# Implied waits left out on TensorE, two pieces of work exchanged, and a loop of four slots, in the second layer of an audio tower

## The chip, the cores and the metric

One Trainium2 chip, one core. The metric is the device time of one execution, in microseconds (us). The program is written in Bass: each engine (PE, the TensorE; DVE, the VectorE; ACT, the ScalarE; POOL, the GpSimd; SP, which issues the DMAs) has its own instruction stream, and the streams meet only at semaphores.

## The reference

The input is 64 sequences of 375 rows of 256 numbers. A first stage makes 188 tokens of each (a convolution of stride 2 and a layer norm), and a first layer adds attention and a quantised feed-forward part. The change touches only the second layer:

```python
q, k, v = heads(x @ wq.T), heads(x @ wk.T), heads(x @ wv.T)      # x is the layer-normed h; 16 heads of 64
phi = lambda t: exp(t @ omega.T - 0.5 * sum(t * t)) / sqrt(64)
out[n] = sum over m <= n of (phi(q)[n] . phi(k)[m]) v[m] / (sum over m <= n of phi(q)[n] . phi(k)[m] + 1e-6)
h = h + out @ wo.T + bo
y = silu(layernorm(layernorm(h)) @ w1 + b1)                     # 1024 columns, w1 and w2 dequantised
h = h + layernorm(h) + 0.5 * (y @ w2 + b2)
```

(The last two lines are in short: the feed-forward part takes the layer-normed h as its input and as its residual.)

## The kernel before

**Slots and chunks.** Layer 2 works on slots of two sequences (32 slots, `SLOTS`), 384 rows each. A slot has eight chunks (`CH`), a chunk being two heads. Chunks are numbered through, g = 8 s + c. Every engine runs the same skeleton, `slots(eng, step)` at L1106: slots -1 to 2 are written out, slots 3 to 28 run in a hardware loop of two slots an iteration (`nc.Fori`, L1116), and slots 29 to 34 are written out again (the last ones only finish work of earlier slots). In the loop the slot number is a register, so a semaphore count that depends on it is worked out by the engine's sequencer; in the written-out slots it is a constant.

**Software pipeline.** In the step of chunk g PE does, in this order (L1332): the omega product of g-1 (`c2_proj`, bank pair B), the q and k products of g (`c1_qk`, bank pair A), the scores of g-2 (`c3_scores`), a piece of "place" 0, the transposes of g-4 (`c5_transpose`), a piece of place 1, the product with V of g-3 (`c4_av`), and a piece of place 2. The pieces are the work that is not done chunk by chunk, and `places` (L1122) writes out by hand which stands where: v in place 0 of the even chunks, wo in place 0 of the odd ones, the eight fc1 pieces of slot s-2, the four fc2 pairs, and the two transposes h5 and xn. All pieces use the two halves of A, as the q and k products do.

**What a piece needs.** Before PE writes a half of A it waits in `bank_free` (L1177) for the last readers, which `read[i]` lists. An fc1 piece f fills both halves with two matmuls each (L1303, L1304). ACT turns half 0 into `pre` (L1405), DVE adds half 1 to it (L1515). One place later ACT takes the tanh (L1413) and DVE multiplies (the gelu-like product, L1522); two places later ACT rounds the result to yT_hi (the copy helper, L1356) and POOL subtracts to get yT_lo (L1594). An fc2 pair j needs both parts of pieces 2j and 2j+1, and DVE adds its result to the rows (L1500). The wait for a pair stands in `fc2_pair` (L1320).

**Precision.** A product of split operands is three matmuls (`product3`, L928, so its lines are L930 to L932): high by low, low by high, high by high. For each chunk ACT copies q and k (qk_hi, twice), DVE subtracts (qk_lo, L1447), ACT squares both (L1365, which counts on qk_hi too), copies the squares (sqs_hi), and POOL subtracts (sqs_lo, L1636, 128x768). The squares are ACT's last reading of A, and they wait for qk_lo.

**Loops of the first layer.** They have the same form (L394), with two tiles an iteration.

Of the kernel before, what the change touches and what calls it, by code (L numbers as in the profile page):

```python
# [16 lines left out]
KC = DM // 128  # L17
# [22 lines left out]
FC = F1 // 128  # L40
# [12 lines left out]
PAIR = 2 * 128  # L53
RING = 4


# [878 lines left out]
def layer1(nc, omega, bo, ln_g, ln_b, fc1_q, fc1_s, fc1_b, fc2_q, fc2_s, fc2_b, h2_dram, out, ident, eps, exponent,  # L935
           w1, w1_memory, w1_loaded):
    GCH = SLOTS * CH
    with ExitStack() as ctx:
# [167 lines left out]
        def slots(eng, step):  # L1106

            last = 3 + (SLOTS - 5) // 2 * 2

            def slot(s, par):  # L1110
                for c in range(CH):
                    step(s, c, par)

            for s in range(-1, 3):
                slot(s, s % 2)
            with nc.Fori(3, last, 2, engines=(eng.engine,), hint_back_edge=True) as s:  # L1116
                slot(s, 1)
                slot(s + 1, 0)
            for s in range(last, SLOTS + 3):
                slot(s, s % 2)  # L1120

        def places(s, par):  # L1122

            p = [[None] * 3 for _ in range(CH)]
            for j in range(4):
                p[2 * j][0] = ("v", s, j)
                p[(2 * j + 7) % CH][0] = ("wo", s if j == 0 else s - 1, j, par if j == 0 else 1 - par)
            for f, (c, n) in enumerate(((2, 1), (2, 2), (3, 1), (4, 1), (4, 2), (5, 2), (6, 1), (7, 2))):
                p[c][n] = ("fc1", s - 2, f)
            p[3][2], p[5][1] = ("fc2", s - 2, 0, par), ("fc2", s - 2, 1, par)  # L1130
            p[0][1], p[1][2] = ("fc2", s - 3, 2, 1 - par), ("fc2", s - 3, 3, 1 - par)
            p[1][1], p[7][1] = ("h5", s - 2), ("xn", s + 1)
            return p
# [13 lines left out]
        with nc.Block() as block:  # L1147
# [26 lines left out]
            def _(pe):  # L1174
# [7 lines left out]
                def c1_qk(s, c, g):  # L1182
                    if c == 0:
                        wait(pe, "xT_hi", s + 1, KC)
                        wait(pe, "xT_lo", s + 1, KC)
                    for i, w in enumerate((wq, wk)):
# [4 lines left out]
                        last.then_inc(S["qk_done"], 1)  # L1191
                        read[i].extend((("qk_hi", 4 * g + (3 + i)), ("qk_lo", 2 * g + (1 + i))))

                def c2_proj(g):

                    wait_g(pe, "qk_lo", g + 1, 2)
                    wait_g(pe, "sq_lo", g + 1)
# [8 lines left out]
                def c3_scores(g, b):  # L1206
                    wait_g(pe, "phi_ready", g + 1)
                    wait_g(pe, "aT_ready", g)
# [16 lines left out]
                def c4_av(g, b, sg, c):  # L1225
                    wait_g(pe, "aT_ready", g + 1)
                    wait_g(pe, "att1_step", g, 3)
                    if c % 2 == 0:
# [22 lines left out]
                def c5_transpose(g):  # L1251
                    wait_g(pe, "att1_step", g + 1, 3)
                    wait_g(pe, "attT_hi", g)
                    wait_g(pe, "attT_lo", g)
# [24 lines left out]
                def xn_transpose(s):  # L1279
# [6 lines left out]
                    for k in range(KC):  # L1286
                        read[k].extend((("xT_hi", s * 2 + (k + 1)), ("xT_lo", s * 2 + (k + 1))))

                def h5_transpose(s):
                    wait(pe, "h5_gb", s + 1, 2)  # L1290
                    transpose_rows(x4, "hT_transposed")
                    for k in range(KC):
                        read[k].extend((("hT_hi", s * 2 + (k + 1)), ("hT_lo", s * 2 + (k + 1))))

                def fc1(s, f):

                    if f == 0:
                        wait(pe, "hT_hi", s + 1, KC)
                        wait(pe, "hT_lo", s + 1, KC)
# [20 lines left out]
                def fc2_pair(s, j, par):  # L1320
                    pe.wait_ge(S["y_hi"], s * FC + (2 * j + 2))
                    pe.wait_ge(S["y_lo"], s * FC + (2 * j + 2))
                    rows_product(s, yT, fc2, j, "fc2_done", "out_ready")

                def wo_pair(s, j, par):
                    pe.wait_ge(S["attT_hi"], s * CH + (2 * j + 2))
                    pe.wait_ge(S["attT_lo"], s * CH + (2 * j + 2))
# [362 lines left out]
```

## Time and profile before

| | |
|---|---|
| time of the runs | 4787.19, 4795.0, 4800.82 us (median 4795.0) |
| the profiled execution | 4793.58 us by its own time, span 4791.8 us, mean granted clock 0.98 |
| PE busy | 93% of the span |
| PE weight loads | 83% |
| DVE, ACT, POOL busy | 71%, 52%, 39% |
| chain that ended last | PE 45%, issue 9%, POOL 5%, DVE 2%, ACT 1% |

The profile is that of one execution. PE is the engine of the matmuls; PEld is its weight loads, which run beside the matmuls before them. Matmuls are pipelined, so a matmul's duration is longer than the distance from its start to the next one's: 0.28 us and 0.12 us for the common 256-column matmul. "issue" as a releaser means that the engine waited for nothing that the profile shows, its sequencer apart. An entry with a q behind the engine's name belongs to its sequencer: branches, register work, waits. An idle time in square brackets is the time that the engine stood still before that row, with what ended it. A cause named for a wait on several semaphores is the one that came last by the profile. The granted clock is a share of 2.4 GHz; the lower level is 1.2 GHz.

### The profile page before, as it was taken

Reading aid. Unit: us, or ns where it says so; the run is one execution under the profiler, and the core shown is the slowest. Engines: PE = TensorE matmul, PEld = TensorE weight load, DVE = VectorE, ACT = ScalarE, POOL = GpSimd, SP = SyncE. Lnnn points to the kernel's source line nnn. Section 1 sums busy time; section 2 is a strip of 40 time slices with the busy share of each in tenths; the row PEclk is TensorE's granted clock in tenths of the full one; section 3 lists DMA queues with packets and bytes.
Section 4 is the critical chain, followed back from the end, with each engine's and each line's share of the span. In section 5 each row is a group of like instructions: output and inputs, shape, how many; then the busy total and the mean of one; then the engine's idle time right before and its main releaser. Section 6 shows DMA issues by size and latency. Waiting matters only on the chain.

```text
span 4791.8 us, 120275 instructions
## 1 busy us (share of the span) xinstructions
PE 4454.1 (93%) x43016; PEld 3973.3 (83%) x43016; DVE 3397.0 (71%) x7197; ACT 2495.3 (52%) x5314; POOL 1855.2 (39%) x2018
## 2 busy tenths in 40 slices
PE   3999999999999948999999999999999999999997
PEld 2888888888888847888888888888888888888886
DVE  5899999999999853666666666665666666666665
ACT  2555555555555524555554554554555555555553
POOL 1444444444444422343343343333334333334333
PEclk9999999999999979999999999999999999999998
DMA  2000000000000010000000000000000000000000
GB/s 82 19 23 23 23 23 23 23 23 23 23 23 23 22 41 8 5 15 8 8 11 11 8 8 15 8 8 15 8 8 11 11 8 8 14 8 8 15 5 11
DMA packets 64881, 78.93 MB, mean 16 GB/s; under 512 B 8759, under 2 KB 51127, under 8 KB 64439
## 3 DMA queue, kind: packets, MB, share of 16 engines
q1 hardware_dynamic: 64566, 74.07, 5.4%
q8 instruction: 279, 4.57, 0.4%
q14 instruction: 36, 0.29, 0.0%
HBM read 49.40 MB, written 24.64 MB: 15 GB/s over the span
## 4 chain that ended last, share of the span: by engine, by line
PE 45%; issue 9%; POOL 5%; DVE 2%; ACT 1%; POOLq 0%; DMA 0%; DVEq 0%; ACTq 0%; SPq 0%
PE bA L930 9%; PE bA L931 8%; PE bA L932 8%; PE bS L1216 3%; PE bO L1239 2%; PE bA L1303 2%; PE bB L930 2%; POOL sqs_lo L1636 2%; PE bB L1202 2%; PE bB L932 2%; PE bB L931 2%; PE bB L1203 2%; PE bA L1304 1%; PE bT L1256 1%; POOL yT_lo L1594 1%
## 5 line engine op out<-in xcount | busy, mean ns | idle before, releaser
L1636 POOL TENSOR_TENSOR sqs_lo<-sq,sqs_hi 128x768 fp32r<-128x768 f32 x256 | 471.4, 1842 | 811.7 <-ACT sqs_hi L1356 803.9
L1447 DVE TENSOR_TENSOR qk_lo<-bA,qk_hi 128x384 fp32r<-128x384 f32 x512 | 283.4, 553 | 626.4 <-ACT qk_hi L1356 626.2
L1375 ACT ACTIVATE phi<-bB 128x768 f32<-128x768 f32 x256 | 207.9, 812 | 681.2 <-PE bB L1203 681.2
L1594 POOL TENSOR_TENSOR yT_lo<-tanh_y,yT_hi 128x384 fp32r<-128x384 f32 x256 | 258.2, 1009 | 631.2 <-ACT yT_hi L1356 631.2
L1356 ACT ACTIVATE qk_hi<-bA 128x384 fp32r<-128x384 f32 x512 | 251.2, 491 | 229.6 <-PE bA L932 229.6
L1457 DVE TENSOR_TENSOR aT<-bS,mask 128x1024 f32<-128x1024 f32 x256 | 310.9, 1215 | 1.8 <-PE bS L1221 1.6
L930 PE MATMUL bA<-fc_lo,yT_hi 128*128 128x256 f32 x768 | 231.5, 301 | 60.9 <-POOL yT_lo L1594 34.2
L1365 ACT ACTIVATE sq<-bA 128x384 f32<-128x384 f32 x512 | 250.2, 489 | 61.7 <-DVE qk_lo L1447 61.6
L516 PE MATMUL bank<-down_sb,hqT 128*128 128x256 f32 x1128 | 278.5, 389 | 1.0 <-ACT hqT L598 1.0
L614 ACT ACTIVATE kblk<-gu,kb_masked,rowmask 128x128 f32<-128x128 f32 x752 | 270.7, 462 | 6.3 <-PE gu L540 6.3
L516 PEld LDWEIGHTS bank<-down_sb,hqT 128*128 128x128 f32 x1128 | 204.4, 190 | 52.6 <-issue 32.6
L930 PE MATMUL bB<-qk_lo,omega_hi 128*128 128x384 f32 x512 | 184.2, 360 | 67.5 <-issue 64.9
L930 PE MATMUL bA<-wo_lo,attT_hi 128*128 128x256 f32 x768 | 226.8, 295 | 18.1 <-DVE qk_lo L1447 5.3
L930 PE MATMUL bA<-wv_lo,xT_hi 128*128 128x256 f32 x768 | 228.4, 297 | 13.2 <-ACT sq L1365 1.0
L1216 PE MATMUL bS<-phi 64*64 64x192 f32 x4096 | 226.5, 337 | 0.0
L1239 PE MATMUL bO<-V,aT 128*64 128x65 f32 x4096 | 219.4, 228 | 0.0
L931 PE MATMUL bA<-fc_hi,yT_lo 128*128 128x256 f32 x768 | 219.3, 286 | 0.0
L932 PE MATMUL bA<-fc_hi,yT_hi 128*128 128x256 f32 x768 | 219.3, 286 | 0.0
L1522 DVE SCALAR_TENSOR_TENSOR tanh_y<-tanh_y,pre 128x384 f32<-128x384 f32 x256 | 214.1, 836 | 6.5 <-ACT tanh_y L1413 6.5
L1303 PE MATMUL bA<-hT_lo,fc_w 128*128 128x384 f32 x512 | 211.7, 414 | 6.6 <-ACT pre L1405 5.4
L1405 ACT ACTIVATE pre<-bA,fc1b,fc1s 128x384 f32<-128x384 f32 x256 | 170.9, 668 | 89.7 <-PE bA L1304 89.6
L931 PE MATMUL bA<-wv_hi,xT_lo 128*128 128x256 f32 x768 | 215.5, 281 | 0.0
(243 smaller groups left out, 15025.4 us busy)
## 6 DMA issues: line engine op xcount, KB each, us to landing
xT<-in_x SPq DMA_DIRECT2D x94, 256.0 KB, 2.7
h_scratch<-h SPq DMA_DIRECT2D x188, 64.0 KB, 1.9
hx<-h_scratch SPq DMA_DIRECT2D x32, 256.0 KB, 2.7
out<-res SPq DMA_DIRECT2D x32, 256.0 KB, 2.1
hx<-h_scratch SPq DMA_DIRECT2D x64, 64.0 KB, 2.4
out<-res SPq DMA_DIRECT2D x64, 60.0 KB, 1.8
q<-in_fc_q SPq DMA_DIRECT2D x2, 1024.0 KB, 6.2
wq_sb<-in_wq SPq DMA_DIRECT2D x1, 1024.0 KB, 5.0
```

Source lines behind the costliest of these rows:

```text
L516: last = pe.matmul(cv[:, 0:DM], hqT[0:w, f, :], down_sb[0:w, f, :], start=f == 0, stop=f == len(F0C) - 1)
L614: act.activation(kblk[:, c, :, j, :], src, ACT.Identity, bias=kb_masked[:, c, j:j + 1], scale=rowmask[:, j:j + 1]).then_inc(S["qk_copied"], 1)
L930: pe.matmul(out, lhs[0], rhs[1], start=start, stop=False)
L931: pe.matmul(out, lhs[1], rhs[0], start=False, stop=False)
L932: return pe.matmul(out, lhs[0], rhs[0], start=False, stop=stop)
L1216: pe.matmul(SC[o:o + 64, h, q], phi[b][p, 1, k], phi[b][p, 0, q], start=True, stop=True)
L1239: pe.matmul(O[o:o + 64, dst(i)], aT[b][:, h, HEADS[i] + o:HEADS[i] + o + 64], V[:, i, v], start=True, stop=True)
L1303: pe.matmul(A[:, k, 0:NT], w, hT[1][:, k, :], start=True, stop=False)
L1447: dve.tensor_tensor(dst, src, hi.bitcast(fp32), ALU.subtract).then_inc(S[done], 1)
L1457: dve.tensor_tensor(aT[b][:], SC[:, :, 0:ST], mask[:].unsqueeze(1).broadcast_to([128, 2, ST]), ALU.mult)\
L1594: pool.tensor_tensor(yT[1][:, f % RING, :], tanh_y[f % 2][:], yT[0][:, f % RING, :].bitcast(fp32), ALU.subtract).then_inc(S["y_lo"], 1)
L1636: pool.tensor_tensor(sqs[1][:], sq[:], sqs[0][:].bitcast(fp32), ALU.subtract).then_inc(S["sq_lo"], 1)
```

## The change

Three things are done in the second layer.

1. The loop takes four slots an iteration. `last` becomes 27, so there are 6 iterations, and slots 27 and 28 are written out.
2. In `places` the fourth fc1 piece (f = 3) moves from chunk 4, place 1 to chunk 3, place 2, and the first fc2 pair moves the other way. The engines all read this table, so ACT, DVE and POOL move their share with it.
3. On PE, waits are left out where another wait of PE's, earlier or at the same place, cannot end before them: those for xT_hi, hT_hi, attT_hi and y_hi beside those for the low part, which is computed from the high one; qk_lo beside the later counts of qk_hi and sq_lo; phi_ready in the scores; and att1_step in the product with V.

```diff
+UNROLL = 4
...
-            last = 3 + (SLOTS - 5) // 2 * 2
+            last = 3 + (SLOTS - 5) // UNROLL * UNROLL
...
-            with nc.Fori(3, last, 2, engines=(eng.engine,), hint_back_edge=True) as s:
-                slot(s, 1)
-                slot(s + 1, 0)
+            with nc.Fori(3, last, UNROLL, engines=(eng.engine,), hint_back_edge=True) as s:
+                for u in range(UNROLL):
+                    slot(s + u, (1 + u) % 2)
...
-            for f, (c, n) in enumerate(((2, 1), (2, 2), (3, 1), (4, 1), (4, 2), (5, 2), (6, 1), (7, 2))):
+            for f, (c, n) in enumerate(((2, 1), (2, 2), (3, 1), (3, 2), (4, 2), (5, 2), (6, 1), (7, 2))):
                 p[c][n] = ("fc1", s - 2, f)
-            p[3][2], p[5][1] = ("fc2", s - 2, 0, par), ("fc2", s - 2, 1, par)
+            p[4][1], p[5][1] = ("fc2", s - 2, 0, par), ("fc2", s - 2, 1, par)
...
                 def c1_qk(s, c, g):
                     if c == 0:
-                        wait(pe, "xT_hi", s + 1, KC)
                         wait(pe, "xT_lo", s + 1, KC)
...
-                        read[i].extend((("qk_hi", 4 * g + (3 + i)), ("qk_lo", 2 * g + (1 + i))))
+                        read[i].append(("qk_hi", 4 * g + (3 + i)))
...
                 def c2_proj(g):
-                    wait_g(pe, "qk_lo", g + 1, 2)
                     wait_g(pe, "sq_lo", g + 1)
...
                 def c3_scores(g, b):
-                    wait_g(pe, "phi_ready", g + 1)
+                    if not has_chunk(g + 1):
+                        wait_g(pe, "phi_ready", g + 1)
                     wait_g(pe, "aT_ready", g)
...
                 def c4_av(g, b, sg, c):
                     wait_g(pe, "aT_ready", g + 1)
-                    wait_g(pe, "att1_step", g, 3)
...
                 def c5_transpose(g):
                     wait_g(pe, "att1_step", g + 1, 3)
-                    wait_g(pe, "attT_hi", g)
...
-                        read[k].extend((("xT_hi", s * 2 + (k + 1)), ("xT_lo", s * 2 + (k + 1))))
+                        read[k].append(("xT_lo", s * 2 + (k + 1)))
...
-                        read[k].extend((("hT_hi", s * 2 + (k + 1)), ("hT_lo", s * 2 + (k + 1))))
+                        read[k].append(("hT_lo", s * 2 + (k + 1)))
...
                     if f == 0:
-                        wait(pe, "hT_hi", s + 1, KC)
                         wait(pe, "hT_lo", s + 1, KC)
...
-                    pe.wait_ge(S["y_hi"], s * FC + (2 * j + 2))
                     pe.wait_ge(S["y_lo"], s * FC + (2 * j + 2))
...
-                    pe.wait_ge(S["attT_hi"], s * CH + (2 * j + 2))
                     pe.wait_ge(S["attT_lo"], s * CH + (2 * j + 2))
```

## Rows read from the trace of the kernel before

**Rows 1.** The page, its first part: busy time and instructions of each engine.

```profile
PE 4454.1 (93%) x43016; PEld 3973.3 (83%) x43016; DVE 3397.0 (71%) x7197; ACT 2495.3 (52%) x5314; POOL 1855.2 (39%) x2018
```

**Rows 2.** What PE waited for in the second layer: us in total, times, longest us.

```profile
PE bB L930 <- issue: 52.0, 48, 3.7
PE bA L930 <- POOL yT_lo L1594: 28.1, 17, 2.2
PE bA L930 <- DVE pre L1515: 22.9, 13, 1.8
```

**Rows 3.** L1116's branch: count, ns min/median/max, first and last start in us.

```profile
L1116 PEldq COMPARE_BRANCH  x13: 88/2137/3497, 2218.3 to 4428.0; - x13
...
L1116 DVEq COMPARE_BRANCH  x13: 55/61/68, 2219.5 to 4429.0; - x13
```

**Rows 4.** The first layer's loop branch, L394, on PE's queue.

```profile
L394 PEldq COMPARE_BRANCH  x42: 80/216/260, 210.7 to 1619.3; - x42
```

**Rows 5.** One loop iteration, second layer then first: busy (x instructions) PE, PEld, DVE, ACT, POOL.

```profile
2405.00:2587.30 182.30, 174.44 (x1816) 160.82 (x1816) 115.59 (x243) 93.30 (x176) 69.75 (x54) 0.99 0.04 10
...
245.50:279.30 33.80, 33.64 (x284) 28.57 (x282) 30.46 (x68) 19.98 (x52) 15.54 (x24) 1.00 0.09 23
```

**Rows 6.** PE in time (start us, us): first product of chunks 7 and 2, three crossings.

```profile
2208.15 0.41 PE L930 MATMUL bB<-qk_lo,omega_hi 128*128 128x384 f32 x1 [0.49 <-issue]
...
2245.43 0.34 PE L930 MATMUL bB<-qk_lo,omega_hi 128*128 128x384 f32 x1
...
2303.28 0.41 PE L930 MATMUL bB<-qk_lo,omega_hi 128*128 128x384 f32 x1 [0.51 <-issue]
...
2336.45 0.34 PE L930 MATMUL bB<-qk_lo,omega_hi 128*128 128x384 f32 x1
...
4233.35 0.41 PE L930 MATMUL bB<-qk_lo,omega_hi 128*128 128x384 f32 x1 [0.49 <-issue]
...
4272.03 0.34 PE L930 MATMUL bB<-qk_lo,omega_hi 128*128 128x384 f32 x1
```

**Rows 7.** The stretch at one edge; granted clock third from last.

```profile
2587.30:2598.00 10.70, 7.03 (x48) 5.83 (x46) 2.92 (x7) 2.79 (x5) 3.63 (x2) 0.84 0.02 5
```

**Rows 8.** PE in time, chunks 3 to 5 of one slot.

```profile
2535.87 0.29 PE L1221 MATMUL bS<-phi 64*64 64x64 f32 x8
2536.27 0.38 PE L930 MATMUL bA<-wo_lo,attT_hi 128*128 128x256 f32 x1
...
2540.59 0.29 PE L1248 MATMUL bO<-V,aT 128*64 128x65 f32 x4
2542.49 0.36 PE L930 MATMUL bA<-fc_lo,yT_hi 128*128 128x256 f32 x1 [1.61 <-POOL yT_lo L1594]
...
2544.62 0.34 PE L930 MATMUL bB<-qk_lo,omega_hi 128*128 128x384 f32 x1
...
2552.18 0.42 PE L1303 MATMUL bA<-hT_lo,fc_w 128*128 128x384 f32 x1
...
2553.16 0.45 PE L1239 MATMUL bO<-V,aT 128*64 128x65 f32 x8
...
2562.70 0.36 PE L930 MATMUL bA<-fc_lo,yT_hi 128*128 128x256 f32 x1
...
2564.99 0.45 PE L1239 MATMUL bO<-V,aT 128*64 128x65 f32 x8
```

**Rows 9.** PE in time, an unrolled slot: end of chunk 0's scores, start of its v.

```profile
4432.98 0.29 PE L1221 MATMUL bS<-phi 64*64 64x64 f32 x8
4433.31 0.39 PE L930 MATMUL bA<-wv_lo,xT_hi 128*128 128x256 f32 x1
```

**Rows 10.** DVE and ACT in time beside that chunk 3.

```profile
2539.04 1.72 DVE L1522 SCALAR_TENSOR_TENSOR tanh_y<-tanh_y,pre 128x384 f32<-128x384 f32 x1
...
2541.98 0.62 DVE L1515 SCALAR_TENSOR_TENSOR pre<-bA,fc1s,pre 128x384 f32<-128x384 f32 x1 [0.75 <-ACT pre L1405]
...
2541.22 0.65 ACT L1405 ACTIVATE pre<-bA,fc1b,fc1s 128x384 f32<-128x384 f32 x1
```

## The prediction

> **What bounds the kernel now.** I began with the page's busy times [rows 1]: PE is busy 4454.1 us of the span of 4791.8, no other engine over 71%. PE sets the end, and the gain must come from its idle time, its slow stretches and its order of work. The change touches only the second layer, from about 1860 us on. Next I read what PE waited for there [rows 2]. Two things stand out: 51.0 us (28.1 + 22.9, 30 times) ahead of an fc2 product, put down to POOL's yT_lo and to DVE's pre, and 52.0 us ahead of the omega product at a chunk's start, put down to "issue", which means that PE's own sequencer was late. The longest of these is 3.7 us. Third I read the loop's own instructions [rows 3]. PE's COMPARE_BRANCH takes 2137 ns in the median and up to 3497; the single short one, 88 ns, belongs to leaving the loop. On DVE it takes 61 ns. Last I went through single slots in order of time [rows 6, 8], as everything there repeats from slot to slot within a few hundredths of a us.
>
> **Part 1, four slots in an iteration.** There are 32 slots; the loop runs from slot 3 to 29 in 13 iterations, so PE jumps back 12 times. After the change it runs from 3 to 27 in 6 iterations and jumps back 5 times: 7 jumps fewer. To price a jump I measured from the first product of chunk 7 to that of chunk 2 in the next slot. Without a jump this takes 2336.45 - 2303.28 = 33.17 us. With one it takes 37.28 at the first jump and 38.68 at the last, so 4.1 and 5.5 us more [rows 6]. Over the 12 jumps the extra is 3.6 to 6.2, mean 4.9. That is more than the branch alone: the register work after it, a second short bubble in the chunk that follows, and at 8 of the 12 jumps a stretch at the lower clock (granted clock 0.84 over the 10.7 us that begin at one jump; of the two levels 1.2 and 2.4 GHz that is a mixture), while PE stood still for up to 3.7 us just before [rows 2, 7]. 7 x 4.9 = **34 us less**; ends 7 x 3.6 = 25 and 7 x 6.2 = 43. Slots 27 and 28 become unrolled code, which costs nothing: unrolled slots take as long as loop slots without a jump.
>
> A longer body could have a price of its own. One iteration holds 1816 matmuls and 1816 weight loads on PE, against 284 and 282 in the first layer's [rows 5], whose jump takes 216 ns [rows 4]. A small body jumps cheaply, a large one doesn't, and nothing in the rows says that it gets dearer once it is large. I take the five that stay at their present price.
>
> The Trainium skill has a rule that speaks against this part (Runtime: NRT & Kernel Launch, "Instruction fetch mechanics"): an engine holds 512 instructions, PE 2048, and a taken branch whose target is no longer held has to fetch it before the engine goes on. Both PE rows agree with it. By it the jumps of DVE and ACT, whose bodies double, would begin to stall as PE's do; that is the second rival below.
>
> **Part 2, waits left out.** Each wait that goes is implied by one that stays, so no order changes; what is saved is sequencer work, and only where PE stands still for it. That is one place in each chunk: the v or wo product after the scores, which needs bank A and so ACT's last read of it. There PE waits for qk_hi first and for qk_lo after it. In the loop 0.40 us lie between the last group of score matmuls and the wo product (2535.87 to 2536.27) [rows 8]. In an unrolled slot, where no count is worked out in a register, it is 0.33 us (4432.98 to 4433.31) [rows 9]. I take 0.07 us for a chunk in the loop, since with one wait left the count can be worked out before it is due. In chunks 3 and 6 the gain is lost again, as PE waits there for DVE or POOL anyway. So 6 chunks x 0.07 x 24 loop slots = 10 us, and about 5 us for the wo products of the 8 unrolled slots, which drop two waits: **15 us less**. Ends: nothing at all, if the instruction that works out the count still stands ahead of the weight load, and 25 us, if waits ahead of fc1 and the omega product were also costing a little.
>
> The waits ahead of the scores, the av product and the transposes are passed while the matmuls before them still run, at no time of PE's. Left out they give nothing; had they hidden work, nothing would be late, since the engine queue is full.
>
> **Part 3, fc2's first pair and fc1's fourth piece change places.** In chunk 3 the fc2 pair follows the av product with 1.61 us of idle [rows 8]. It needs yT_lo of piece 1, which comes by a chain: DVE's gelu product on tanh_y ends at 2540.76 (2539.04 + 1.72) [rows 10], then ACT rounds it, and then POOL subtracts. After the change fc1's piece 3 stands there. It needs no yT, but it needs bank A, which fc1's piece 2 has just filled: half 0 is free when ACT's pre ends, 2541.22 + 0.65 = 2541.87, half 1 when DVE's pre ends, 2541.98 + 0.62 = 2542.60 [rows 10]. ACT's pre stands behind the rounding of the same piece 1, so the chain only loses its last link. The first matmul comes at about 2541.97, the one for half 1 at 2542.65, and the next chunk 0.46 later, at 2543.11. From the last av group (2540.59) that is 2.52 us instead of 4.03 (2544.62) [rows 8]. In chunk 4 the fc1 piece took 0.98 us (2552.18 to 2553.16); the fc2 pair in its place will take what the pair of chunk 5 takes, 2.29 (2562.70 to 2564.99) [rows 8], since by then its yT is long there. Before: 4.03 + 0.98 = 5.01; after: 2.52 + 2.29 = 4.81. So 0.20 us in this slot. The other slots by the same working give 0.17 to 0.40, apart from three in which the clock fell; I take 0.3 x 30 slots = **9 us less**. The stall is not gone, it is late for another reason: ACT's and DVE's pre. Ends: 0, and the whole 51.
>
> The three slots in which the clock fell after this stall took, between the marks of [rows 8], some 0.9 to 1.6 us longer than the others. With less idle time some stay at full clock: **2.5 us less**, ends 0 and 5.
>
> DVE and POOL in chunk 4: DVE gets the gelu product of piece 3 and the two additions of the fc2 pair, as it has in chunk 5 now, where PE's next fc1 starts on time. I cost it at nothing; the cover is the av product between them, and without it about 0.2 us a slot, 6 in all.
>
> **Sum.** 34 + 15 + 9 + 2.5 = 60.5 us. The profiled execution took 4793.6 us by its own time (span 4791.8), the median of the runs is 4795.0, so they are the same for this purpose. 4793.6 - 60.5 = 4733.
>
> **Rivals.**
>
> *A, the jumps that stay get dearer.* If a jump's price goes with the length of the body, the five cost 9.7 each: 12 x 4.9 - 5 x 9.7 = 10 us saved instead of 34, and the time is 4757. For it: large body dear, small body cheap. Against: twelve jumps of one length say nothing of a slope. Chance 0.1.
>
> *B, the jumps of DVE and ACT begin to stall.* DVE's 243 instructions in an iteration, its sequencer's own not counted [rows 5], become 486. DVE reaches its jump 1.2 us after PE [rows 3]. A stall of PE's length there (2.1 to 3.5 us) ends 3.3 to 4.7 us after PE's jump began. DVE is first needed once PE has got through its own stall (2.1), the register work (0.5), the omega product (1.7), the q product (1.1) and ACT has copied that (0.5): about 5.9 us after. So it is covered, unless the fetches hold each other up: 2 to 3.5 us x 5 = 10 to 17 us back, 4746. Here hangs the skill's rule named above. Chance 0.15 for a cost that can be seen.
>
> *C, the waits left out give nothing* and the rest holds: 4748. Chance 0.1.
>
> *D, the stall of chunk 3 goes altogether*, because ACT gets to its pre earlier: another 30 to 40 us, about 4697. Against it: the order of ACT's work ahead of pre is not touched. Chance 0.05.
>
> *E, slower: DVE falls behind in chunk 4.* Its gelu product takes 1.72 us in chunk 3 [rows 10], beside POOL's long subtraction, though pre, of the same size, takes 0.62. The one of piece 3 moves from a quiet place to the start of chunk 4, beside the same subtraction. If the additions behind it then free bank A late, fc1's piece 4 and chunk 5's products stall as chunk 3 does, twice 1.6 us in each of 30 slots, 96 us more: 4829. It turns the sum's sign from 60.5 / 30 = 2.0 us a slot on, and is slower by over 0.3% from 2.5. Against it: chunk 5 has this very order today without a stall. Chance 0.04.
>
> The forecast has the remaining 0.56. Its own range, from the ends of the terms (25 to 43, 0 to 25, 0 to 15 for the swap as reckoned, 0 to 5), not all at one end together, is 4713 to 4755. Cases A to C reach 4757; the range goes to 4708 and 4762, which leaves out D, E and a little more. A measurement of this kernel tells about 0.3%, 14 us, from no change. Faster by more than that: all but E and a thin rest, 0.94; within it 0.03; slower 0.03.
>
> **What would show it.** PE's branch at L1116 seven times fewer, 5 long ones, still near 2 to 3.5 us; if near 5, A. DVE's branch no longer near 60 ns: B. From the last score group to v or wo 0.33 us instead of 0.40: part 2; 0.40 still: C. At chunk 3 PE's wait is ahead of L1303, put down to pre, of 1 to 1.2 us; chunk 4's fc2 without a wait. A wait ahead of fc1 in chunk 4 for the additions of L1500 would be E. Wrong altogether would be a time above 4762 or under 4708.

## The result, and the profile after

The changed kernel takes 4708.8 us in the median of four runs (4706.8 to 4712.3), against 4792.2 us for the kernel before: a ratio of 0.9825, 95% interval 0.9808 to 0.9842. The profiled execution's span is 4706.4 us, 85.4 less than before. The forecast was 4733, with a range of 4708 to 4762. Direction and order of size were right; the gain was 83 us where 60 were forecast, and the time lies 0.8 us above the low end of the range.

The page's first part and the granted clock in 40 slices:

```profile
PE 4433.3 (94%) x43016; PEld 3957.0 (84%) x43016; DVE 3392.2 (72%) x7197; ACT 2497.9 (53%) x5314; POOL 1856.4 (39%) x2018
...
PEclk9999999999999987999999999999999999999998
```

PE is busy 21 us less than before [rows 1], though it does the same matmuls (43016 both times). A matmul's duration grows at the lower clock, and in the stretch from 1860 to 4640 us the clock, which before stood at its lower level for 51 us in all, never fell.

What PE waited for in the second layer (us in total, times, longest us), to be held against [rows 2]:

```profile
PE bA L1300 <- ACT pre L1400: 36.3, 32, 1.2
PE bB L931 <- POOL sqs_lo L1631: 20.7, 36, 1.2
PE bB L931 <- issue: 7.9, 5, 1.6
```

The waits before fc2 are gone but for some 2 us. 36.3 us now stand ahead of fc1's matmul L1300 and are put down to ACT's pre, as the prediction said they would be. The 20.7 us before the omega product are the wait of chunk 7 for POOL, which was there before under the name "issue". Without these, "issue" has shrunk from about 31 us to 7.9.

The loop's branch on PE and DVE, to be held against [rows 3]:

```profile
L1117 PEldq COMPARE_BRANCH  x6: 88/1810/1866, 2391.8 to 4169.6; - x6
...
L1117 DVEq COMPARE_BRANCH  x6: 61/68/68, 2393.2 to 4170.8; - x6
```

Five long branches of PE, as forecast. But the longest takes 1866 ns, where twelve before took 1837 to 3497. DVE's branch is where it was.

A slot's seam on PE, from the first product of chunk 7 to that of chunk 2, without a jump and then with one, as in [rows 6]:

```profile
2293.34 0.45 PE L931 MATMUL bB<-qk_lo,omega_hi 128*128 128x384 f32 x1 [0.44 <-POOL sqs_lo L1631]
...
2326.29 0.34 PE L931 MATMUL bB<-qk_lo,omega_hi 128*128 128x384 f32 x1
...
2381.91 0.45 PE L931 MATMUL bB<-qk_lo,omega_hi 128*128 128x384 f32 x1 [0.44 <-POOL sqs_lo L1631]
...
2416.65 0.34 PE L931 MATMUL bB<-qk_lo,omega_hi 128*128 128x384 f32 x1
```

Without a jump 32.95 us, with one 34.74: a jump costs 1.8 us. The five cost 1.5 to 1.8, mean 1.7. Before it was 4.9.

Chunks 3 and 4 of one slot on PE, as in [rows 8], with DVE and ACT beside chunk 3, as in [rows 10]:

```profile
2608.49 0.29 PE L1221 MATMUL bS<-phi 64*64 64x64 f32 x8
...
2608.82 0.39 PE L931 MATMUL bA<-wo_lo,attT_hi 128*128 128x256 f32 x1
...
2613.08 0.29 PE L1247 MATMUL bO<-V,aT 128*64 128x65 f32 x4
...
2614.55 0.44 PE L1300 MATMUL bA<-hT_lo,fc_w 128*128 128x384 f32 x1 [1.18 <-ACT pre L1400]
...
2615.27 0.44 PE L1300 MATMUL bA<-hT_lo,fc_w 128*128 128x384 f32 x1
...
2615.74 0.34 PE L931 MATMUL bB<-qk_lo,omega_hi 128*128 128x384 f32 x1
...
2623.18 0.36 PE L931 MATMUL bA<-fc_lo,yT_hi 128*128 128x256 f32 x1
...
2625.42 0.39 PE L1238 MATMUL bO<-V,aT 128*64 128x65 f32 x6
```

```profile
2611.52 1.86 DVE L1517 SCALAR_TENSOR_TENSOR tanh_y<-tanh_y,pre 128x384 f32<-128x384 f32 x1
...
2614.60 0.62 DVE L1510 SCALAR_TENSOR_TENSOR pre<-bA,fc1s,pre 128x384 f32<-128x384 f32 x1 [0.75 <-ACT pre L1400]
...
2613.42 0.52 ACT L1351 ACTIVATE yT_hi<-tanh_y 128x384 fp32r<-128x384 f32 x1 [1.42 <-DVE tanh_y L1517]
...
2613.84 0.65 ACT L1400 ACTIVATE pre<-bA,fc1b,fc1s 128x384 f32<-128x384 f32 x1
```

From the last scores to the wo product 0.33 us, where it was 0.40. From the last av group (2613.08) to the next chunk (2615.74) 2.66 us, where 4.03 stood and 2.52 were forecast. The fc2 pair in chunk 4 takes 2.24 us to the av product (2623.18 to 2625.42), forecast 2.29. ACT's pre ends at 2614.49, and PE's fc1 starts 0.06 later.

**Where 85 us went.** Three sums, all read from the two traces. (1) Jumps: 12 x 4.87 = 58.4 us before, 5 x 1.69 = 8.5 after, so 50. (2) A slot that holds no jump and runs at full clock: 89.42 us before, 88.53 after (the sum of its eight chunks' medians). 0.89 x 30 = 27. (3) The falls of the clock behind the stall of chunk 3 in three slots, about 4. About 4 are left. The time from the start of slot 30 to the end fell from 273.0 to 269.4 us, but part of that is in term (2) already, so these last 4 are only partly placed.

Terms (2) and (3) are the forecast's parts 2 and 3. Term (1) is 16 us larger than forecast, because the jumps that stayed got cheaper. The experiments ask why.

### The profile page after: what moved, and what is told of

Its sections match the earlier page's. It is cut to its first block, busy times and chain, and to the rows that moved or that the text cites. A ratio compares the mean times of both kernels' runs of the same rounds, so it can differ in the third digit from the quotient of the medians.

```text
span 4706.4 us, 118165 instructions
## 1 busy us (share of the span) xinstructions
PE 4433.3 (94%) x43016; PEld 3957.0 (84%) x43016; DVE 3392.2 (72%) x7197; ACT 2497.9 (53%) x5314; POOL 1856.4 (39%) x2018
## 4 chain that ended last, share of the span: by engine, by line
PE 49%; issue 5%; DVE 3%; POOL 3%; ACT 2%; POOLq 0%; DMA 0%; DVEq 0%; ACTq 0%; SPq 0%
PE bA L931 10%; PE bA L932 8%; PE bA L933 8%; PE bS L1216 4%; PE bO L1238 2%; POOL sqs_lo L1631 2%; PE bB L931 2%; PE bA L1300 2%; PE bB L1202 2%; PE bB L1201 2%; PE bB L933 2%; PE bB L932 2%; DVE tanh_y L1517 1%; PE bT L1254 1%; PE bA L1301 1%
## 5 line engine op out<-in xcount | busy, mean ns | idle before, releaser
L1300 PE MATMUL bA<-hT_lo,fc_w 128*128 128x384 f32 x512 | 210.2, 410 | 47.3 <-ACT pre L1400 43.1
L1351 ACT ACTIVATE sqs_hi<-sq 128x768 fp32r<-128x768 f32 x256 | 214.8, 839 | 1.2
```

The lines of the kernel that those rows point to most:

```text
L1300: pe.matmul(A[:, k, 0:NT], w, hT[1][:, k, :], start=True, stop=False)
L1351: act.activation(dst, src, ACT.Copy).then_inc(S[done], 1)
```

## The experiments

The experiments ran in three groups, 1 to 4, then 6, 7, 9 and 10, then 5, 8, 11 and 12, each on one chip with the kernel before beside them (medians 4792.8, 4793.0 and 4797.6 us). Between groups the ratios to the kernel before are the better comparison; the changed kernel's is 0.9825. I counted instructions on PE, the sequencer's included, along the trace. "A jump" is always the extra over an undisturbed seam, "a slot" an undisturbed slot.

What started them: in the trace of before the bubbles after a jump are not spread. In this one, the first of the loop, PE stands still before the omega product, and again before the first q product:

```profile
2221.15 0.44 PE L930 MATMUL bB<-qk_lo,omega_hi 128*128 128x384 f32 x1 [2.37 <-issue]
...
2224.45 0.44 PE L930 MATMUL bA<-xT_lo,wq_hi 128*128 128x384 f32 x1 [1.30 <-issue]
```

In 8 of the 12 jumps the second bubble comes ahead of the same instruction, the 26th after the branch. Where it doesn't, it is mostly the branch itself that took 3.2 to 3.5 us. These eight bubbles are a row of PE's waits in the second layer that stands right behind [rows 2]:

```profile
PE bA L930 <- issue: 8.4, 8, 1.5
```

The page's DMA part of before shows how code arrives (queue, packets, MB, share):

```profile
q8 instruction: 279, 4.57, 0.4%
```

16 KB a packet. The traces also hold each packet with its start and its end. In a stretch of straight code (run 12 below, 2100 to 4500 us) 199 of them start, one for each 256.1 instructions of PE. So the theory was that PE reads its code in blocks of 256 instructions, and that the price of a jump depends on where in its block the loop's first instruction and the branch back happen to lie. The change moves both: waits left out ahead of the loop shift its start by 80 instructions, and the body's length moves the branch.

**1. The loop of four slots alone.**

```diff
# from the kernel before; nothing else
+UNROLL = 4
-            with nc.Fori(3, last, 2, ...) as s:
+            with nc.Fori(3, last, UNROLL, ...) as s:
```

> Only the loop of four slots; waits and places as before. In the trace of the changed kernel a jump of PE costs 1.6 to 1.8 us beyond an undisturbed seam, against 3.2 to 5.8 (mean 4.9) before. My theory: the price hangs on where the loop's first instruction lies in PE's instruction stream. Before, the 26th instruction after the jump comes 0.9 to 1.6 us late in 8 of 12 jumps, and where it doesn't, the branch itself takes 3.2 to 3.5 us, as if a second block of code had to be fetched. The waits left out ahead of the loop shift its start by 80 instructions. Theory: the start is not shifted here, so 5 jumps at 4.9 each, 34 us less than before: about 4758, with the second bubble at the 26th instruction. Rival (a body of four slots makes the jump cheap): 5 jumps at 1.7, 50 us less: about 4742. Rival (the waits at the seam made it cheap): as the theory, but without a fixed place of the bubble.

4750.7 us, ratio 0.991 (0.9893 to 0.9926). The branch of PE, and one jump in time:

```profile
L1117 PEldq COMPARE_BRANCH  x6: 88/1534/1925, 2399.0 to 4211.4; - x6
...
2401.41 0.44 PE L931 MATMUL bB<-qk_lo,omega_hi 128*128 128x384 f32 x1 [1.92 <-issue]
...
2404.41 0.44 PE L931 MATMUL bA<-xT_lo,wq_hi 128*128 128x384 f32 x1 [1.00 <-issue]
```

The second bubble is there, at the 26th instruction again. A jump costs 2.9 to 5.4, mean 3.6. Neither number was met: the long body doesn't make a jump cost 1.7, and the unshifted start doesn't keep it at 4.9. The second bubble stayed with the unshifted start; the branch itself got cheaper by something else, and in this kernel it stands elsewhere in its block.

**2. Everything but the loop: waits and places, two slots an iteration.**

```diff
# from the changed kernel
-UNROLL = 4
+UNROLL = 2
```

> Waits left out and places exchanged, the loop at two slots as before, so 12 jumps. The start of the loop is shifted as in the changed kernel. Theory: 12 jumps at 1.7 instead of 4.9, 38 us less, and some 0.9 us a slot from waits and places, 27 us, and 3 from the clock: about 4724. Rival (the body of four slots makes the jump cheap): jumps at 4.9, so 30 us less: about 4762.

4709.8 us, ratio 0.9832 (0.9816 to 0.9849): as fast as the changed kernel, with 12 jumps instead of 5.

```profile
L1117 PEldq COMPARE_BRANCH  x13: 88/452/1514, 2216.1 to 4346.9; - x13
```

A jump costs 0.54. So beside the other two parts the loop of four slots was worth nothing: 12 x 0.54 = 6.5 us against 5 x 1.69 = 8.5. The rival of the long body falls here. The theory was right in direction, but far too careful: I had taken 1.7 from the changed kernel, and its branch has a bad place.

**3. The kernel before, its code only shifted by 176 instructions.**

```diff
             def _(pe):
+                for _ in range(176):
+                    pe.sem_inc(S["pad"], 1)
                 read = [[], []]
```

> The kernel before, and nothing but 176 semaphore increments of PE at the start of the second layer, where PE stands still for some 40 us for its first data; they move the loop's start by 176 instructions, to the place in a block of 256 that it has in the changed kernel (80 fewer, which is 176 more). Theory: the 12 jumps cost 1.7 each instead of 4.9, the second bubble is gone: 38 us less, about 4754. Both rivals: no change, 4792, or a little slower by what the increments cost.

4775.6 us, ratio 0.996 (0.9946 to 0.9975). All twelve branches now take 357 to 371 ns, and there is no second bubble:

```profile
L1116 PEldq COMPARE_BRANCH  x13: 88/357/371, 2240.3 to 4400.8; - x13
```

A jump costs 0.68 instead of 4.87, which is 50 us less for the twelve. Not all of it reaches the time, because the increments were not free as I had thought. PE stood still 59.8 us before its first matmul instead of 39.8:

```profile
PE bA L1286 <- issue: 59.8, 1, 59.8
```

The first slot starts 20.8 us later. 50 - 21 = 29; the two profiled spans differ by 26.5. The medians differ by 17 only (38 were forecast): the profiled run is one of two at 4766 to 4767 us, the other three took 4776 to 4779, and no trace says what those 10 us are. No wait, place or slot was touched here, and the twelve jumps of the trace agree within 0.14 us, so what moves a jump from 4.9 to 0.7 us is the place of the code and nothing else.

The same trace shows why the increments cost time. Of the long idle time before the first matmul only the last 7.3 us (1782.3 to 1789.6) lie behind the last point at which PE meets the other engines. The increments begin there, run one after the other, 0.151 us each, and end 0.11 us ahead of the first matmul: 26.6 us of work in 7.3 us of room.

**4. The changed kernel, shifted back by 80.**

```diff
             def _(pe):
+                for _ in range(80):
+                    pe.sem_inc(S["pad"], 1)
```

> The changed kernel with 80 such increments, which bring the loop's start back to its old place. Theory: 5 jumps at 4.9 instead of 1.7, 16 us more than the changed kernel: about 4725, with the late 26th instruction back. Both rivals: as the changed kernel, 4709.

4715.2 us, ratio 0.9838 (0.9821 to 0.9854). The bubble at the start of the loop is back, ahead of the same q product (the 27th instruction by the same count), but the branch is now short:

```profile
L1117 PEldq COMPARE_BRANCH  x6: 88/362/418, 2400.6 to 4178.3; - x6
...
2401.38 0.44 PE L931 MATMUL bB<-qk_lo,omega_hi 128*128 128x384 f32 x1 [0.26 <-issue]
...
2404.67 0.43 PE L931 MATMUL bA<-xT_lo,wq_hi 128*128 128x384 f32 x1 [1.30 <-issue]
```

A jump costs 1.75, as in the changed kernel, but made up the other way round: there a branch of 1.8 us and no bubble, here a branch of 0.4 and a bubble of 0.8 to 1.6. The time is 6 us over the changed kernel's. The idle time before the first matmul grew from 39.9 to 45.0 us by the increments; the next slot starts 8.7 us later, of which 1.7 were there before the increments began. The forecast of 4.9 a jump was wrong, and this told what was missing: start and branch have a price each.

**5. The changed kernel, shifted by 60**, as 4 with 60 for 80, after the other experiments had given the two distances below.

> The changed kernel with 60 semaphore increments of PE at the start of the second layer, which shift the loop's code by 60 instructions. In it the loop's start lies 106 instructions ahead of the end of its block of 256, and the jump back stands 59 behind the start of its own. With the shift they are 46 and 119. Theory: a jump is cheap when both distances are large enough; the branch falls from 1.8 to 0.4 us and no second bubble comes. The increments themselves cost about 6 us once, before the first slot, as 80 cost 8.7 and 176 cost 20.8. Rival: the branch stays at 1.8, since the long body causes it.

One run, 4706.2 us, with a profile and no interval. The branch:

```profile
L1117 PEldq COMPARE_BRANCH  x6: 88/362/418, 2396.2 to 4168.1; - x6
```

A jump costs 0.3 us and no bubble comes, with the body of 7589 instructions that the changed kernel has. The long body is not the cause. The five jumps save 7 us and the increments cost some 4 (forecast 6), so the time hardly moves.

Put together, with the two distances in instructions (the block edge is taken from the late 26th instruction of before and carried to the others by counting, so it may be off by one or two in all of them alike; the forecast of 5 has 106 and 46 for 105 and 45):

| kernel | start of loop to the end of its block | start of its block to the branch | branch ns | second bubble | a jump, us |
|---|---|---|---|---|---|
| before | 25 | 18 | 1837 to 3497 | in 8 of 12 | 4.87 |
| loop of four alone | 25 | 36 | 1477 to 1925 | yes | 3.56 |
| changed, shift 80 | 25 | 139 | 357 to 418 | yes | 1.75 |
| changed | 105 | 59 | 1640 to 1866 | no | 1.69 |
| waits alone (6) | 105 | 117 | 361 to 1888 | no | 1.08 |
| all but the loop (2) | 105 | 116 | 357 to 1514 | no | 0.54 |
| changed, shift 60 | 45 | 119 | 357 to 418 | no | 0.32 |
| before, shift 176 | 105 | 194 | 357 to 371 | no | 0.68 |
| one wait alone (8) | 73 | 194 | 357 to 371 | no | 0.56 |

The first distance decides the bubble, the second the branch. The packets in the traces show how.

- An iteration has as many packets as its body touches blocks of 256 by these distances: 17 before (25 + 15 x 256 + 18), 31 in the changed kernel, 32 with the loop of four alone, 16 in 2 and 6.
- The traces of the kernels with a loop hold 107 jumps. The 57 branches of over 1.3 us all end 1.34 to 1.60 us after the landing of the last packet before their end. Ahead of the 50 short ones (0.36 to 0.46 us) that packet had started 2.4 to 8.3 us before the branch.
- The instruction behind the second bubble comes 1.2 to 1.6 us after the landing of the next packet, which starts 0.7 to 1.35 us after the branch's end (34 jumps: before, 1, 4 and 7).
- How early the first of these packets starts goes with the branch's place: 139 instructions into its block 5.1 to 5.7 us ahead of the branch, 59 into it 0.8 to 1.0 ahead, and in the kernel before, at 18, between 0.6 ahead and 0.7 behind. At 116 and 117 it is 2.4 to 3.9 us ahead in some jumps and 0.4 to 1.0 in others; what decides between them stays open.

So the branch waits for the packet of its target, and the second bubble for the packet behind it. A branch near the start of its block comes before the first has landed; a loop that starts near the end of its block runs into the second one too soon. What the hint has to do with it, run 9 shows.

**6. The waits alone**, and **7. the places alone.**

```diff
# 6: from the changed kernel, UNROLL = 2 and the old places:
-            ... (3, 1), (3, 2), (4, 2) ...      p[4][1] = ("fc2", s - 2, 0, par)
+            ... (3, 1), (4, 1), (4, 2) ...      p[3][2] = ("fc2", s - 2, 0, par)
# 7: from the kernel before, the same two lines the other way
```

> Before, with PE's waits left out and nothing else: 12 jumps, fc2's first pair in chunk 3. The waits do two things. They shorten an undisturbed slot (89.4 us) by 0.07 us in each chunk that doesn't wait elsewhere, some 0.5 us, 15 us in all. And they move the loop's code, start and end, to where the kernel with waits and places has it, so the 12 jumps cost 0.5 each instead of 4.9, 52 us. Theory: about 4725. Rival, by which waits are worth only what they cost where they stand: about 4777.

> Before, with fc1's fourth piece and fc2's first pair exchanged and nothing else; no instruction is added ahead of the loop's start or in its body, so the jumps keep their 4.9 us. An undisturbed slot gets 0.3 us shorter (chunks 3 and 4 together 23.9 to 23.6), and the three falls of the clock behind this stall go: 9 + 3 = 12 us, about 4780. Rival, the whole stall gone: 4740.

The waits alone: 4730.9 us, ratio 0.9865 (0.9848 to 0.9882). A slot takes 88.81 us, 0.61 less, and a jump 1.08, which makes 18 + 45 us. More than two thirds of what leaving out waits brought in this kernel came from the code's place. The forecast of 0.5 for each of the twelve jumps was too low: six branches are long (1.3 to 1.9 us) and six short.

The places alone: 4771.4 us, ratio 0.9949 (0.9932 to 0.9966), 22 us less where 12 were expected. Chunks 3 and 4 together went from 23.89 to 23.52 us, as expected within 0.1, and a slot to 88.92, 0.5 shorter, of which 0.1 I can't place. PE's wait has changed its name:

```profile
PE bA L1303 <- ACT pre L1405: 31.8, 29, 1.8
```

A jump cost 5.15 in the profiled run. That run was the slowest of its four, 4781 against 4769 to 4773 in the other three; so the trace accounts for its own run's 12 us, and the 10 us more of the median stay open: the other three runs have no trace. Jumps that differ from run to run would do it, but that isn't shown.

**8. One wait alone**: qk_lo ahead of the first write into A.

```diff
-                        read[i].extend((("qk_hi", 4 * g + (3 + i)), ("qk_lo", 2 * g + (1 + i))))
+                        read[i].append(("qk_hi", 4 * g + (3 + i)))
```

> Before, with only qk_lo left out ahead of a piece's first write into bank A (the line in the q and k products), all other waits kept. Part 2 of the prediction puts the gain of the waits, where they stand, at this one place. In the trace: 0.33 us instead of 0.40 from the last group of scores to v or wo in the loop, an undisturbed slot 0.4 to 0.5 us shorter (89.4 to 88.9). What the run's time does depends besides on where the code ahead of the loop and of the branch now ends, 4.9 or 0.5 us a jump, so I forecast the slot and not the time. Rival, the gain is spread over all waits: the slot at 89.3.

4732.8 us, ratio 0.9861 (0.9845 to 0.9878), the same as all the waits together. From the start of the last score matmul to that of v or wo it is 0.255 us instead of 0.331, in all eight chunks, and a slot takes 88.81 us, as with all the waits left out. So part 2's claim holds for the slots in the loop: of the waits left out only this one was in PE's way. It also moves start and branch to a good place, and the twelve jumps cost 0.56:

```profile
L1116 PEldq COMPARE_BRANCH  x13: 88/357/371, 2220.9 to 4368.3; - x13
```

**9. Without the hint.**

```diff
-            with nc.Fori(3, last, UNROLL, engines=(eng.engine,), hint_back_edge=True) as s:
+            with nc.Fori(3, last, UNROLL, engines=(eng.engine,), hint_back_edge=False) as s:
```

> The changed kernel with the hint of the second layer's loop switched off, on all engines; the computation is the same. Theory: the hint is what keeps the jumps of DVE (876 instructions in the body) and ACT (728) at 60 and 49 ns, and what makes PE's 1.8 us and not more. Without it DVE's and ACT's branches take over 1 us and PE's 3 to 4, so a jump costs 2 us more, 10 us in all: about 4719. Rival, the hint does nothing here: 4709, branches as before.

4726.2 us, ratio 0.9857 (0.984 to 0.9873), 15 us slower than the changed kernel by the ratios.

```profile
L1117 PEldq COMPARE_BRANCH  x6: 82/3602/3867, 2393.1 to 4187.3; - x6
...
L1117 ACTq COMPARE_BRANCH  x6: 40/45/57, 2393.4 to 4187.6; - x6
...
L1117 DVEq COMPARE_BRANCH  x6: 55/63/81, 2394.4 to 4188.6; - x6
```

PE's branch takes 3.6 us and a jump 4.95. The branch records of ACT and DVE stay short, against what I expected, but the stall stands behind them: ACT's next instruction comes 2.5 to 2.8 us after the branch, where it came 0.4 after it with the hint, and DVE's next register instruction after 2.8 to 3.0 instead of 0.6. Both are covered, since ACT next waits for PE's omega product anyway.

PE's packets show what the hint does. One packet still starts 0.5 to 1.1 us ahead of the branch, but now a further one starts 1.0 to 1.3 us behind the branch's start, and the branch ends 1.34 to 1.38 us after that one lands. An iteration has 32 packets instead of 31. So without the hint the packet ahead of the branch isn't that of the target, and with the hint it is.

For ACT and DVE the rule of the Trainium skill (Runtime: NRT & Kernel Launch, "Instruction fetch mechanics"), by which a jump to code that an engine no longer holds has to fetch it, agrees with the trace: ACT's 710 and DVE's 857 instructions from one branch to the next are over the 512 that it gives them. The second queue of code on the page, of the kernel before and then of the changed one, fits too:

```profile
q14 instruction: 36, 0.29, 0.0%
...
q14 instruction: 119, 0.97, 0.1%
```

In the traces of before and of 2, with two slots an iteration, none of its 8 KB packets starts between the loop's branches. With four slots (1 and the changed kernel) it is 14 an iteration, and without the hint 17. What this run adds is that the hint hides most of the stall.

**10, 11. Two versions that go on from there.** PE's wait in chunk 3 is for ACT's pre of fc1's piece 2, which stands behind the rounding of piece 1, and that waits for DVE. The first version lets ACT take pre first in this one place; the second also lets DVE take its addition before attT_lo there.

```diff
# ACT, place():
+                    first = (c, n) == (3, 1)
+                    if first:
+                        run_place(dict(fc1=fc1), s, c, n, par)
                     run_place(dict(fc1=fc1_y), s, c, n, par, 2)
                     run_place(dict(fc1=fc1_tanh), s, c, n, par, 1)
-                    run_place(dict(v=v_pair, fc1=fc1, ...), s, c, n, par)
+                    if not first:
+                        run_place(dict(v=v_pair, fc1=fc1, ...), s, c, n, par)
# 11, DVE, step(): place 1 ahead of ec5 when c == 3
+                    if c == 3:
+                        place(s, c, 1, par)
                     if has_chunk(g - 4):
                         ec5(g - 4, (c - 4) % CH)
-                    place(s, c, 1, par)
+                    if c != 3:
+                        place(s, c, 1, par)
```

> The changed kernel; in chunk 3, place 1 ACT takes fc1's piece 2 (pre) ahead of rounding piece 1, not after it. Theory: what holds PE in chunk 3 now is ACT's pre, queued behind the rounding, which waits for DVE's gelu product. Then the first matmul of fc1's piece 3 follows the av product in 0.15 us instead of 1.41, and only its second half waits, for DVE's pre, which gets 0.8 us earlier: 0.8 us a slot, 23 us less, about 4686, the wait now put down to DVE. Rival, DVE's pre comes no earlier because DVE is the one that is late: no change, 4709.

> The kernel with ACT's pre ahead of the rounding in chunk 3, and now DVE's addition into pre (piece 2) ahead of the attention's subtraction attT_lo in the same chunk too. What held PE in chunk 3 after the first of these was DVE's pre (15 us in 30 slots). Theory: it comes 0.55 us earlier, the second half of fc1's piece 3 starts some 0.45 us earlier, 14 us in all: about 4668. Rival, DVE's later work now delays the transposes or the fc2 pair: no gain, 4681.

The first takes 4681.5 us, ratio 0.9764 (0.9748 to 0.9781). What is left of PE's waits before fc1:

```profile
PE bA L1300 <- DVE pre L1514: 14.9, 30, 0.5
...
PE bA L1300 <- ACT pre L1400: 3.2, 3, 2.4
...
PE bA L1300 <- DVE res L1499: 0.3, 1, 0.3
```

DVE's pre has taken over, 0.5 us at most, apart from three waits. Chunk 3 went from 11.89 to 11.04 us. The second takes 4668.4 us, ratio 0.9729 (0.9713 to 0.9745), chunk 3 10.58, and PE's waits in the second layer are now these:

```profile
PE bB L931 <- POOL sqs_lo L1638: 20.8, 36, 1.2
PE bB L931 <- issue: 7.4, 5, 1.8
PE bA L931 <- DVE pre L1514: 0.6, 1, 0.6
```

Both forecasts held within 5 us. This is the fastest of the kernels with a loop, 40 us under the changed one, or 46 by the ratios.

**12. The same, all slots written out.**

```diff
-            for s in range(-1, 3):
-                slot(s, s % 2)
-            with nc.Fori(3, last, UNROLL, ...) as s:
-                ...
-            for s in range(last, SLOTS + 3):
+            for s in range(-1, SLOTS + 3):
                 slot(s, s % 2)
```

> The same with no loop in the second layer: all slots written out, so no jump at all. 5 jumps at 1.6 go, 8 us; counts of semaphores are constants, by which an undisturbed slot changed by less than 0.3 us in the written-out slots. Theory: 4660, at most 8 us either way. Rival, straight code is fetched too slowly: slower than with the loop, with PE's waits put down to issue in the middle of slots.

4666.8 us, ratio 0.9728 (0.9712 to 0.9744), no different from 11 by the intervals. No wait is put down to issue:

```profile
PE bB L931 <- POOL sqs_lo L1633: 20.6, 36, 1.2
PE bA L931 <- ACT pre L1395: 1.1, 2, 0.6
```

Straight code is fetched in time here. A slot takes 87.36 us instead of 87.20, 0.16 x 24 = 4 us more: in a written-out slot the wo product starts 0.347 us after the last score matmul, in the loop 0.255, and chunks 1, 5 and 7 are 0.06 to 0.07 us longer. Against that stand the five jumps of 11, which in its profiled run cost 1.3 to 3.5 us, mean 2.3, with the clock falling behind two of them. The profiled spans differ by 5.2 us, the medians by 1.6.

## Why the prediction was right, and where it was off

**PE bounds, and its idle time is what can be had:** right. Every part that helped did so on PE.

**What bounds, a reading.** 52.0 us of "issue" ahead of the omega product were read as PE's own sequencer being late. 36 of those 48 waits, some 20 us, are chunk 7's wait for POOL, which the change left as it was.

**Part 1, the loop: right sign, and its price was mis-sized.** The step that failed is "I take the five that stay at their present price". 12 jumps at 4.9 were measured correctly, 34 us for seven of them was right as far as it goes, but the five that stayed fell to 1.7. 58.4 - 8.5 = 50 us. Nor is it the number of jumps that saved this time: with the other two parts in place, 12 jumps cost 6.5 us and 5 cost 8.5 (2), so what the prediction put down to fewer jumps came, beside them, from where the edits moved the code. Alone, the loop of four saves 42 us (1). The prediction's reason, "a small body jumps cheaply, a large one doesn't", was also wrong: with bodies of 3884 and 7589 instructions a jump costs 0.3 to 0.7 us, if start and branch lie well in their blocks (3 and 5), and with the same 3884 it costs 4.9, if they lie badly. The row that could have told it was in the trace of before: 8 second bubbles, all at one instruction. The prediction names this bubble and adds it to the price without asking why it is always there.

**Part 2, the waits: the place and the size of one were right,** 0.40 to 0.33 us, shown by the run with one wait. The reason was only half right. The 0.07 us came from setting a wo product in the loop beside a v product in an unrolled slot, and the difference was put down to counts worked out in a register. In that v product the trace has qk_lo's wait first, passed 0.86 us early, and the late one, for qk_hi, on the weight load itself. An unrolled wo product, with no count to work out either, took 0.46 us from the last score matmul, and 0.35 without the two waits. What costs is the late wait standing as an instruction of its own ahead of another. That the number fitted was in part luck. 15 us were forecast; a slot gained 0.61 us where 6 x 0.07 = 0.42 were reckoned. The distance shrank by 0.076 us in all eight chunks. In chunk 3 the gain was lost, as forecast (13.48 to 13.45). Chunk 6 gained, against the forecast (10.18 to 10.06 in the run with the waits alone), though it ends in a wait for POOL's sqs_lo; why, I did not try.

**Part 3, the exchange: right.** 0.3 us a slot forecast, 0.31 between the kernels with the waits (88.81 to 88.50), and the remaining stall at the named place with the named cause, 1.18 us. That this cause was ACT's order of work was then shown by changing the order (10): the stall shrank to 0.5 us. The clock's falls behind this stall went too; in the kernels with the exchange, between 1870 us and the last slots, it fell only right behind long jumps, but for one fall in 2.

**The rivals.** A, dearer jumps with a longer body: no, cheaper. B, stalls of DVE and ACT: they show without the hint, 2.5 to 3.0 us, and no wait of PE's names them; with the hint they are 0.4 to 0.6. C, nothing from the waits: no. D, the whole stall gone: not by this change, but by 10 and 11, for 40 us, about the size that was given for it. E, DVE falling behind in chunk 4: no, chunk 4 takes 11.6 us, as chunk 5 does (11.7).

**The range** held the time by 0.8 us at its low end, and by luck: the ends of the terms gave 4713, and the step down to 4708 had no term behind it. It had been built from the spread of the jumps' prices seen before, 3.6 to 6.2, and none of the jumps that stayed was in that spread. A bound from a spread says nothing on what moves the mean.

## What to carry to other kernels

When a hardware loop's jump costs an engine microseconds, look at single jumps: how long the branch takes, and whether a second bubble comes at a fixed instruction. If it does, look whether the code's place is what is being paid for, by shifting the code alone; any edit ahead of the loop or in its body changes it, so an edit's own worth must be read from a stretch without jumps. A wait left out is worth something only where the engine stands still between two waits in a row; and when an idle time is moved, ask what stands ahead of its new cause in that engine's order, since a swap of two instructions there was worth as much as a third of this whole change.

## What was unexpected of the hardware

- The place of code. PE's jump back cost 0.3 to 4.9 us in the nine kernels of the table that do the same work at the seam, ordered by two distances to the edge of a block of 256 instructions. 176 added instructions made the twelve jumps 50 us cheaper. Every long branch ended 1.34 to 1.60 us after a packet of code had landed. At 116 to 117 instructions the branch was short in 16 jumps and over 1.3 us in 8; at 119 it was short five times out of five.
- A pure semaphore increment on PE takes 0.151 us. 176 of them at the head of the layer, in what had looked like 40 us of idle time, put off the first matmul by 20, because PE could begin them only 7.3 us before it had been due.
- Two waits in a row cost 0.076 us more than one, when the first is the one that ends late: from ACT's update to the matmul it is 0.12 us in the kernel before, and 0.044 in the changed one, where the weight load itself waits for it.
